# Layer one of a two-layer kernel: RELU kept in PSUM, remainders on VectorE, two norms on ScalarE, the energy addition on GpSimd, steps placed anew

## What is computed

```python
avg = jnp.cumsum(x, axis=1) / jnp.arange(1, l + 1, dtype=x.dtype)[None, :, None]
ci = avg.reshape(b, l, H, d).transpose(0, 2, 1, 3).reshape(b * H, l, d)      # H = 16 heads of d = 16
pc = ci @ W_pe + b_pe
dyn, gate = (pc[..., :K], pc[..., K:])                                       # K = 31 taps
energy = stt + jax.nn.sigmoid(gate) * dyn
w = jax.nn.softmax(energy, axis=-1)
for kk in range(K):
    out = out + w[:, :, kk:kk + 1] * padded[:, kk:kk + l, :]
v = conv_loc @ W_fc.T + residual
v = (v - mu) / jnp.sqrt(var + EPS) * gamma + beta
...
h = relu(hidden_states @ W1 + b1) @ W2 + b2                                  # 256 -> 1024 -> 256
```

## Time and profile before

| | us |
|---|---|
| median of 3 runs | 4125.69 (4121.95 to 4126.24) |
| the profiled execution, its own time | 4126.56 |
| its span in the trace | 4124.8 |
| PE busy in the span | 3587.8 (87%) |
| DVE busy | 3014.8 (73%) |
| ACT busy | 1835.5 (45%) |
| POOL busy | 1463.0 (35%) |

### The profile page before, as it was taken

How to read it: one execution, slowest core, us unless ns; L and a number is a source line. 1 busy time by engine, 2 the same in 40 slices (tenths; PEclk the granted TensorE clock), 3 DMA queues, 4 the chain that set the end, 5 groups by cost and what they waited for, 6 DMA issues and landing times.

```text
span 4124.8 us, 71833 instructions
## 1 busy us (share of the span) xinstructions
PE 3587.8 (87%) x27626; PEld 2939.0 (71%) x27626; DVE 3014.8 (73%) x6429; ACT 1835.5 (45%) x3522; POOL 1463.0 (35%) x1075
## 2 busy tenths in 40 slices
PE   4999999999931599999999269999999999999998
PEld 2888888888821488888888147777777777777777
DVE  4777777777768877677763587888888888888863
ACT  2666666666520255545554123434334334343343
POOL 1223233323220255555554213333333334333333
PEclk7999999999965799999999579999999999999999
DMA  4232222221110333333332364544444555554441
GB/s 169 73 108 96 91 96 76 73 68 63 39 59 0 72 70 78 75 80 81 84 84 32 88 117 102 109 105 100 99 100 104 109 105 107 104 109 105 89 94 37
DMA packets 740869, 355.95 MB, mean 86 GB/s; under 512 B 549162, under 2 KB 693904, under 8 KB 740400
## 3 DMA queue, kind: packets, MB, share of 16 engines
q1 hardware_dynamic: 715952, 316.74, 31.3%
q0 software_dynamic: 24576, 34.62, 4.9%
HBM read 215.35 MB, written 135.92 MB: 85 GB/s over the span
## 4 chain that ended last, share of the span: by engine, by line
PE 68%; DVE 22%; issue 5%; ACT 2%; POOL 1%; DMA 1%; SPq 1%; POOLq 0%; ACTq 0%; DVEq 0%
PE bank L1198 9%; PE bank L739 9%; PE bank L723 9%; PE bank L1214 8%; PE bank L1799 6%; PE bank L1785 5%; PE bank L116 4%; PE bank L1757 4%; PE bank L701 3%; PE bank L1766 2%; PE bank L1739 2%; DVE hits L1031 2%; DVE l_stats L569 2%; DVE x L1676 2%; DVE energies L1637 1%
## 5 line engine op out<-in xcount | busy, mean ns | idle before, releaser
L1491 POOL TENSOR_TENSOR l_hidden_low<-l_hidden_full,l_hidden_high 128x512 fp32r<-128x512 f32 x256 | 373.0, 1462 | 954.6 <-ACT l_hidden_high L1569 954.5
L1140 DVE TENSOR_TENSOR hidden_low<-bank,hidden_high 128x512 fp32r<-128x512 f32 x256 | 174.1, 690 | 289.5 <-ACT hidden_high L985 289.5
L631 DVE TENSOR_TENSOR gT_low<-bank,gT_high 128x512 fp32r<-128x512 f32 x256 | 173.5, 688 | 256.0 <-ACT gT_high L538 255.8
L979 ACT ACTIVATE bank<-bank,fc_bias 128x512 f32<-128x512 f32 x256 | 169.5, 662 | 428.4 <-PE bank L1198 427.2
L1799 PE MATMUL bank<-l_w_high,l_hidden_low 128*128 128x256 f32 x1024 | 314.0, 307 | 49.3 <-POOL l_hidden_low L1491 49.3
L1757 PE MATMUL bank<-bandT,window 128*32 128x96 f32 x5632 | 270.0, 344 | 78.2 <-DVE energies L1634 44.7
L739 PE MATMUL bank<-w_high,gT_low 128*128 128x256 f32 x1024 | 316.0, 309 | 0.6 <-DVE gT_low L631 0.6
L532 ACT ACTIVATE bank<-bank,b 128x512 f32<-128x512 f32 x256 | 169.5, 662 | 318.9 <-PE bank L723 318.8
L1119 DVE TENSOR_TENSOR onehot_p<-bank,slot_p 128x1024 bf16<-128x1024 f32 x256 | 311.0, 1215 | 0.0
L1563 ACT ACTIVATE l_hidden_full<-bank,l_b 128x512 f32<-128x512 f32 x256 | 175.6, 686 | 280.9 <-PE bank L1785 280.7
L1799 PE MATMUL bank<-l_w_high,l_hidden_high 128*128 128x256 f32 x1024 | 294.0, 287 | 0.0
(11 more groups left out here) (300 smaller groups left out, 11303.2 us busy)
## 6 DMA issues: line engine op xcount, KB each, us to landing
bandT<-bands SPq DMA_DIRECT2D x352, 240.0 KB, 3.6
fc_full<-in_L_ffn_fc_wT SPq DMA_DIRECT2D x32, 1024.0 KB, 5.7
bands<-zeros SPq DMA_DIRECT2D x22, 768.0 KB, 8.3
x<-in_L_attn_x SPq DMA_DIRECT2D x32, 512.0 KB, 6.3
moe_output<-zeros SPq DMA_DIRECT2D x32, 512.0 KB, 7.1
x_after_retention<-x SPq DMA_DIRECT2D x32, 512.0 KB, 3.0
moe_input_and_gates<-xn SPq DMA_DIRECT2D x32, 512.0 KB, 4.1
x<-x_after_retention SPq DMA_DIRECT2D x32, 512.0 KB, 4.2
```

Source lines behind the costliest of these rows:

```text
L1140: v.tensor_tensor(t.hidden.low[:, n % SLICES, :], K.banks[t.bank["expand", i, g, 0]][:, :], t.hidden.high[:, n % SLICES, :], ALU.subtract) ...
L1491: e.tensor_tensor(t.hidden.low[:, n % SLICES, :], t.hidden_full[n % 4][:, :], t.hidden.high[:, n % SLICES, :], ALU.subtract).then_inc(s("l ...
```

## The change

- The RELU is written back into its PSUM bank. ACT cuts the high part from the bank, and DVE, no longer POOL, forms the remainder from bank and high part. `hidden_full` is gone. The bank is held until the remainder is done.
- `norm_in` and `norm_x3` are ACT activations with a scale (the root) and a bias (minus mean times root). DVE computes the negated mean as well, in `moments`, and POOL multiplies it with the root (`root_and_center`).
- The step `energies` is split. `gated` is DVE's product; POOL adds the static energy; `energies` on DVE takes maximum and difference.
- Banks 0 to 5 are one pool, given out by the places of the steps (`timed_banks`, which retention used already; retention's own banks come out the same). A kernel product takes an aligned pair.
- Places come from a table of numbers instead of formulas.

Core of the diff:

```diff
-def order_d(C, NT, TT, KF):
+PLACES_D = {
+    "l1_contract": 2.44, "load": (3.0, 10.8), "join": (5.44, 13.37), "stats_in": (6.76, 14.66), "root_in": (7.74, 15.64), "norm_in": (8.51, 16.43),
...
+EXPAND_D = 48.0
+
+BANKS_D = {"turn_in": (2, 0.5), "kernel_product": (2, 0.9), "window_turn": (1, 0.3), "convolve": (1, 0.4), "mix": (1, 0.6), "turn_mid": (2, 0.5),
+           "l1_expand": (1, 1.6)}
...
-BANKS_D = {"turn_in": 2, "kernel_product": 2, "window_turn": 1, "convolve": 1, "mix": 1, "turn_mid": 2}
...
-    t.bank = paired_banks(ordered(K.B, t.steps), BANKS_D, range(4))
+    placed = order_d(KF)
+    t.steps, t.bank = [step for _, *step in placed], timed_banks(K.B, placed, 2 * KF, BANKS_D, range(6), ("kernel_product",))
...
+    def root_and_center(kind, taken, n):
+        if n >= 1:
+            e.wait_ge(s(taken), n)
+        root(kind, n)
+        e.wait_ge(s(f"l1_root_{kind}"), n + 1)
+        e.tensor_tensor(t.center[kind][:, :], t.less_mean[kind][:, :], t.root[kind][:, :], ALU.mult).then_inc(s(f"l1_center_{kind}"), 1)
...
-        elif name == "l1_expand":
-            half, f = args
-            for g in ([f - 1] if f else []) + ([f] if f == KF - 1 else []):
-                n = KF * (2 * b + half) + g
-                e.wait_ge(s("l1_hidden_high"), n + 1)
-                e.tensor_tensor(t.hidden.low[:, n % SLICES, :], t.hidden_full[n % 4][:, :], t.hidden.high[:, n % SLICES, :], ALU.subtract).then_inc(s("l1_hidden_low"), 1)
+        elif name == "energies":
+            n = b * t.C + args[0]
+            e1 = t.e[n % 2]
+            e.wait_ge(s("gated_energy"), n + 1)
+            e.tensor_tensor(e1[:, :, :], e1[:, :, :], t.energy[:, :, :], ALU.add).then_inc(s("full_energy"), 1)
...
+        if name in ("norm_in", "norm_x3"):
+            n = 2 * b + args[0]
+            kind, out, done = ("in", t.moe[n % 2], "l1_xh") if name == "norm_in" else ("x3", t.v[n % 2], "h4")
+            e.wait_ge(s(f"l1_center_{kind}"), n + 1)
+            for k in range(HC):
+                m = e.activation(out[:, k, :], t.x2[n % 7][:, k, :], ACT.Identity, scale=t.root[kind][:, k:k + 1], bias=t.center[kind][:, k:k + 1])
+            m.then_inc(s(done), 1)
...
-            e.activation(t.hidden_full[n % 4][:, :], K.banks[4 + f % 2][:, :], ACT.Relu, bias=t.b1[:, f:f + 1]).then_inc(s("relu"), 1)
+            e.activation(bank[:, :], bank[:, :], ACT.Relu, bias=t.b1[:, f:f + 1]).then_inc(s("relu"), 1)
...
+            v.wait_ge(s("full_energy"), n + 1)
             v.tensor_reduce(top[:, :], e1[:, :, :], AX_X, ALU.max).then_inc(step, c.up())
...
+                v.wait_ge(s("l1_hidden_high"), m + 1)
+                v.tensor_tensor(t.hidden.low[:, m % SLICES, :], K.banks[t.bank["l1_expand", b, half, g, 0]][:, :], t.hidden.high[:, m % SLICES, :],
+                                ALU.subtract).then_inc(s("l1_hidden_low"), 1)
...
-            bank = take(4 + f % 2, "relu", KF * n + f + 1)
+            bank = take(t.bank["l1_expand", b, half, f, 0], "l1_hidden_low", KF * n + f + 1)
```

More of the change, by code:

```diff
@@ L349, in timed_banks @@
         number, hold = wanted.get(name, (0, 0))
-        for k in range(number):
-            bank = min(of, key=lambda b: free[b])
+        if name in paired:
+            first = min(of[::2], key=lambda b: max(free[b], free[b + 1]))
+            taken = [first, first + 1]
+        else:
+            taken = sorted(of, key=lambda b: free[b])[:number]
+        for k, bank in enumerate(taken):
             free[bank] = place + hold
@@ L1289, in layer_one_tiles @@
+            at(slot, "l1_expand", half, f)
+            at(slot + PLACES_D["l1_contract"], "l1_contract", half, f)
+    for name, place in PLACES_D.items():
+        if isinstance(place, tuple):
+            for k, one in enumerate(place):
+                at(one, name, k)
+        elif name != "l1_contract":
+            at(place, name)
+    return [(place + slices * lag, name, lag, *args) for place, _, name, lag, args in sorted(plan, key=lambda z: z[:2])]
 def layer_one_tiles(K, ctx):
@@ L1628, in layer_one_vector @@
             v.tensor_tensor(view, view, t.per_count[:, :], ALU.mult).then_inc(s("avgT"), 1)
[L1629 removed]
+        elif name == "gated":
             (ch,) = args
             n = b * C + ch
[L1632 removed]
+            e1 = t.e[n % 2]
             v.wait_ge(s("gate"), n + 1)
```

124 lines of the change are left out of this document (39 added, 85 removed).

## The result

The changed kernel takes **4002.76 us** (median of 4 runs, 4001.32 to 4007.34) against 4125.97 of the kernel before on the same chip: a ratio of 0.9702, 95% interval 0.9685 to 0.9719. It is 123 us faster, where 49 were forecast; the forecast's range holds it near its lower end. The profiled execution's span is 3999.8 us against 4124.8.

A forecast was written before the change was run, and what follows sets the result against it. PE was taken to bound layer one's turn: 95.1 us floor + 4.6 wait + 2.8 slow clock + 1.6 mid-turn = 104.1, 3.8 below 107.9, times 13 = 49 us. Forecast 4076 us, range 4000 to 4135.

The forecast's parts named there:

- D: PE's 3.1 us wait before a convolution, for a bank held by DVE's gated product; forecast to go.
- B: PE's 1.4 us "issue" wait before a convolution, for a window's copy queued on ACT; forecast to go.
- C: PE's 1.0 us wait for the bank of the output; forecast to go.
- A: PE's 3.5 us wait before a contraction, for POOL's remainder; forecast to stay, at 4.6 us, for DVE's.
- I count neither: my 85.3 keeps today's mean durations.: DVE's load a turn, 85.3 us from 87.4, with no gain or loss from collisions with POOL.
- The middle's 1.6: Mid-turn: a late DVE now and then holds a bank, 1.6 us a turn, bounds nothing and 4.
- The clock then dips behind one wait instead of two; I keep A's 2.8.: PE's slow clock behind the contraction's wait costs 2.8 us a turn; the convolution's 1.5 goes.
- Floor: PE's work at full clock in a layer-one turn, 95.1 us; the change removes no matmul.
- I put both at 0, with bounds of 6 either way.: The first turns, without MLP, and the last turns: no net gain or loss, bounds 6 us.
- rival 1: The wait before the contraction shrinks to 1 us without a dip: 98.0 us a turn, 3997 us; chance 0.16.
- Rivals 2 and 3: 2: waits return in mid-turn, near 4118 us, chance 0.16. 3: the contraction's wait reaches 10.4 us, 4152 us, chance 0.14.
- rival 2: Mid-turn handoffs between DVE and POOL and held banks cost 4 us a turn: near 4118 us; chance 0.16.

The follow-up runs named there:

- e5: The changed kernel with all its new code in the old places (gated at +0.23, energies at +0.70 of each chunk's old place): 4189.50 us.
- e6: The kernel before with only the new places, old banks and engines kept: 4090.15 us.
- e4: The changed kernel with the remainders back on POOL and the RELU in SBUF, the addition staying on POOL: 4115.51 us.
- f14: The changed kernel with 16 added unused subtractions of constants a turn on POOL, which wait for nothing: 4029.74 us.
- e9: The changed kernel with 16 added unused subtractions a turn on POOL at the old remainders' places, each waiting for ACT's high part: 4128.74 us.
- after: The changed kernel itself, against the kernel before: 4002.76 us, ratio 0.9702.
- f15: As e10, but with the exponentials of chunk 7 behind the first window's copy on ACT and the softmax's product later: 3966.91 us.
- e7: The changed kernel with banks dealt as before, 0 to 3 in turn, 4 and 5 for the RELU: 4069.47 us.
- f13: As e9 with the same waits, but POOL's 16 added instructions a turn write zeros and read nothing: 4106.61 us.
- f16: As f15, with the transposed second half moved later on PE, 17.43 to 17.70: 3976.67 us.
- e1: The changed kernel with the entering second half's statistics moved behind the remainders of slices 6 and 7: 4002.09 us.
- e10: The changed kernel with the entering second half's statistics behind remainders 6 and 7, and chunk 7's maximum and difference behind those statistics: 3986.20 us.
- e11: As e10, with the transposed second half moved later on PE, 17.43 to 17.70: 3991.54 us.

## Why the prediction was off

**D, B, C go.** Right: none is left, and no bank is waited for.

**A.** Place and releaser were right, the size was not: 4.6 forecast and 3.2 measured in the mean (3.54 in the turn shown), below the lower bound of 3.7. In that turn the mix began 10.1 us ahead of PE's dry point, where I had 10.55, and the chain from there to the end of the remainder took 13.6 us (3251.24 to 3264.87) where I had 15.2: residual 1.6 for 1.9, softmax 2.0 for 2.4, mix step 1.1 for 1.3, maximum and difference 1.3 for 1.4, twice.

**"I count neither: my 85.3 keeps today's mean durations."** This step failed: DVE took 78.5. Its own instructions got 6.9 us a turn shorter. The load that was taken from POOL had been inside them: with the old places and the new engines (e5) DVE is at 78.0, with the new places and the old engines (e6) at 88.4, and the remainders alone put back on POOL (e4) give back 5.4. f14 gives a price: 17.1 us of reads a turn put back on POOL (167.7 x 101.7 / 1000) made DVE 2.0 us a turn busier and cost 27 us in all. The changed kernel took off 24.1 us of remainders and put on 11.0 of additions. So of the 74 us that the forecast missed, an estimate by f14's price, (24.1 - 11.0) / 17.1 x 27, puts 21 us on this. POOL's busy time alone does not forecast the length: e4 and e6, with POOL at 483 and 402 in 1000, have the long softmax product (1325 and 1425 ns), e9 with 441 has not (1099). It depends on which instructions meet.

**The middle's 1.6.** It is 0. The stretch did not lack time: DVE waits in ten turns 85 us for ACT's high parts and 30 for the mixes' banks, so it has slack where I saw 2 us in 44. I had built that sum of the same long durations. Which of the shorter instructions gave the slack, no run takes apart.

**"The clock then dips behind one wait instead of two; I keep A's 2.8."** The price of a dip was right, but this step failed in taking one for every turn. Three turns of after with the same wait at the edge (3.38, 3.35 and 3.40 us), from first average to first average (PE busy, PEclk, DMA):

```profile
2676.90:2775.80 98.90, 95.52 (x844) 1.00 0.53 114
3378.40:3478.80 100.40, 97.05 (x844) 0.98 0.53 112
3276.50:3378.40 101.90, 98.50 (x843) 0.97 0.52 110
```

PE waits once in each of the 13 turns, 2.9 to 3.5 us. In 6 of them the clock stays at 1.00 and PE is busy 95.6 us in the mean; in the other 7 it falls in the wait or just behind it, and PE is busy 96.8 to 98.6. A dip thus costs 1.2 to 3.0 us, which is PE's busy time in it times the missing clock, less 0.1 to 0.3. Over the 13 turns it is 1.2 us a turn. What decides whether the clock falls behind such a wait, no run shows. f15 has a dip in one turn of 13; of the 2.6 us by which its turn is shorter than after's, 1.6 are the wait and 1.0 the clock.

**Floor.** PE's work at full clock is 95.6 us, in after's 6 turns and in f15's 12 alike, where I had 95.1. The working took off two dips by busy time times the missing clock, which is 0.1 to 0.3 too much for each; by this estimate 0.2 to 0.6 of the floor's error comes from there.

**Sum.** For 95.1 + 4.6 + 2.8 + 1.6 = 104.1 the 13 turns have 95.6 + 3.2 + 1.2 + 0 = 100.0 us. Floor +0.5, A -1.4, clock -1.6, middle -1.6: 4.1 us a turn, 53 us over 13 turns.

**"I put both at 0, with bounds of 6 either way."** This step failed too: the ends gave 22 us (9.2 in the turn before the 13, 11.8 in the tail, the rest 0.7). The tail is 224.7 in e6 and 231.9 in e5, against 235.6 before and 223.8 after, and 239.2 in e7. So the tail is short with the new places where the banks are the new ones or the code is the old. The early turn is 82.9 in e6 and 92.4 in e5 against 86.8 before and 77.6 after: the places again, and most with the new code. These are readings of whole runs; none takes an end apart. I had costed the ends by the work moved between engines and not by the order.

**The rivals.** Of rival 1 the time came (3997 forecast), by luck and not by its mechanism: the edge stayed open at 3.2 us, and the gain came from the middle, from dips that did not come in half of the turns, and from the ends. Rivals 2 and 3 did not come; what e9 and f13 show is near rival 2, waits for POOL in the middle, and happens when POOL keeps the remainders' places in its queue. That the addition could move to POOL depended on the remainders leaving it; the forecast costed the two by load and never as one queue.

**Open.** Why e5 is slower than before: its waits are named, but no run takes its places apart, and the places of `gated` and `energies` in it are my choice, so it prices this one fitting of the new code. How much of the 123 us each mechanism is worth: the 21 us are an estimate, and the parts of the change are not additive (e5, e6). Whether the last 1.6 us a turn of f15 can go was tried once (f16) and not found.

## What to carry over

- Take an engine's queue as an order, not as a load: work moved onto an engine is worth what it is only if nothing ahead of it there waits for something slower. Here 16 more instructions a turn on GpSimd cost 27 us, and with a wait for ScalarE ahead of each 126 (f14 and e9).
- When work leaves GpSimd, the means of VectorE's two-input instructions are no longer to be used; take their shortest undisturbed ones and the means as two ends, and look for new meetings: one instruction that nothing had met before, the difference, got longer by half.
- A wait at the critical engine that is closed by moving one step mostly opens at the next step in the same queues (e1, e10, e11); it was halved only when the queues of VectorE and ScalarE were both followed (f15, 36 us).
- A dip of the clock is priced well by busy time times the missing clock, but count the turns in which it comes: here it was 7 of 13 behind the same wait.

## What the runs showed of the hardware

- A DVE instruction of 128x4 elements took 880 ns in the mean before (the variance of the entering half) and 161 in the changed kernel. Every other one was long: that at 2742.16 took 1.59 us and ended at 2743.75, with POOL's row addition, which ran from 2741.38 to 2743.73. So tiny instructions pay for the neighbour as large ones do. In e9 that of the middle's variance took 1061 ns.
- Behind the same wait of 2.9 to 3.5 us of PE the granted clock fell in 7 of 13 turns of the changed kernel and stayed at 1.00 in 6; PE was busy 95.6 us a turn without a dip and 96.8 to 98.6 with one.
- A neighbour that only writes did not lengthen the one instruction of DVE's with two SBUF inputs that met it alone. In f13 nine of the differences L1636 run while POOL writes zeros and nothing else, and all 74 take 674 to 677 ns. What got longer there met POOL's reads: the scan of the average took 3220 ns in the mean against 2281, and each of the nine long ones (4.06 us at 2805.31) overlaps the row addition (2804.85 to 2807.22); the ten long softmax products (mean of all 1126 against 1041) overlap the join.
